# Last layers of a graph network: whole float32 features against a count matrix that GpSimd's queue widens while it loads

## The chip, the cores and the metric

The program runs on one core of a Trainium2 chip. The metric is the device time of one execution in microseconds; lower is better. The kernel before was run three times.

## The reference

A graph of 6250 nodes with 128 features and 106,250 edges (self loops among them) passes through four blocks, each followed by a residual add and a layer norm: an attention layer, a dense block with edge sums, three attention layers, and at the end five layers (GIN) that this case is about:

```python
for l in range(5):
    agg = jax.ops.segment_sum(h[src], dst, num_segments=N)
    rst = h + agg
    x = rst @ W1[l] + b1[l]
    x = jax.nn.relu(_bn(x, bn1_g[l], bn1_b[l]))
    x = x @ W2[l] + b2[l]
    x = jax.nn.relu(_bn(x, bn2_g[l], bn2_b[l]))
    h = jax.nn.relu(_bn(x, bn3_g[l], bn3_b[l]))
```

`_bn` normalises each feature over all nodes. The edges are the same in all five layers.

## The kernel before

The nodes are 49 blocks of 128 (`NB`), padded to 50 (`NBP`). Features live either with nodes on the partitions (`X`, `S`) or with features on the partitions (`XTa`, `XTb`).

**The count matrix.** The segment sum of the last five layers is done as a dense product. `adjacency()` (lines 1493 to 1562) builds, once, how often each source node feeds each destination node. The destinations are cut into 13 windows (`NWIN`) of 504 columns (`WD`; the last has 224), the sources into the 49 blocks, which gives 637 (`NKEY`) panels of 128 x 504. TensorE adds up one-hot products in PSUM (line 1516). DVE makes the one-hots (1523, 1526). ScalarE copies two panels at a time to float16 (1549), zeroes the banks (1551) and stores the pair (1539), in a hardware loop over the pairs. In HBM each panel is 128 rows of 504 float16 values. In the first half of this stage GpSimd gathers rows for another layer on its queue (lines 1196 to 1213).

**One layer** is `neighbours(l)` (from 1564), then `linear`, `relu_norm`, and `split_features(False)` (1783), which turns the result back to nodes on partitions for the next layer. Between phases stands a barrier of all engines (`end_phase`).

- The features are held as three bf16 parts whose sum is the float32 value (`H3`): ScalarE rounds to the first part (1807), DVE subtracts and rounds to the second (1812, 1814), GpSimd subtracts for the third (1817).
- Lines 1586 to 1590 compute 52 sums of features for edges that the matrix leaves out (`extra`, the extra counts), and lines 1591 to 1603 split those into three parts too (`V3`).
- The main loop (1605 to 1630) goes over the windows in two parts: windows 0 to 6 (3528 columns), then 7 to 12 (2744 columns), one PSUM bank for each window. For each of the 49 source blocks it takes one tile of counts (line 1622, the three bf16 parts one after the other) and adds the block's own features by an identity (1625).
- A tile is loaded by SyncE's queue (`load_tile`, 1777), in 7 or 6 panels of 1008 bytes a partition. There are five tile buffers (`NT`), three of them in `XTb`, and the first two tiles of a layer (`KEPT`) are loaded during the phase before. A load waits for the product of the tile five before it.
- Line 1636 adds the extra sums. DVE and ScalarE then evict the windows (1645, 1648). The first dense weights (1583, float32) are multiplied window by window within the second part's matmuls, one window every five blocks, and at the end for the second part; ScalarE adds the bias (1651) and DVE takes statistics.

Before the first layer, `run_hit` is built by an iota and a comparison (1770, 1772) and `split_features(True)` splits `X`. After the fifth layer `feature_to_node` (894) turns the features back with transposes (873), an activation (901) and a copy (907), and a layer norm and the store of the output follow.

Of the kernel before, what the change touches and what calls it, by code (L numbers as in the profile page):

```python
# [19 lines left out]
F32 = mybir.dt.float32  # L20
BF16 = mybir.dt.bfloat16
F16 = mybir.dt.float16
# [59 lines left out]
NT = 5  # L82
# [21 lines left out]
def build(nc, a, out):  # L104
    ctx = ExitStack()
    with ctx:
# [19 lines left out]
        adj = dram("adjacency", (2 * PAIRS, P, WD), F16)  # L126
# [4 lines left out]
        S = sb("state", NBP * C)  # L131
        XTa = sb("xT_a", NP)
        XTb = sb("xT_b", NP)
        steptab = sb("step_table", 3 * KS, I32, 1)
        act_tab = sb("act_table", 2 * KT, I32, 1)
        freetab = sb("free_table", T // TG, I32, 1)
        fresh = sb("new_block", KP)
        src_cols = sb("src_cols", ET)
        dst_cols = sb("dst_cols", ET)
# [6 lines left out]
        Wext = sb("w_ext", 4 * (D + 2))  # L146
# [10 lines left out]
        src_idx = sb("src_idx", ET, I32)  # L157
        step_col = sb("step_col", KJ)
        run_dst = sb("run_dst", 1)
        extra = sb("extra_counts", NV * NBP, F16)  # L160
# [5 lines left out]
        def gsb(name, cols, dt=F32):  # L166
            return gat_only.enter_context(nc.sbuf_tensor(name, [P, cols], dt))
# [31 lines left out]
        for name in ("chain", "load", "load2", "store", "stage", "mm", "evac", "out",  # L199
# [4 lines left out]
                     *[f"ld{h}" for h in range(NT)], *[f"st{h}" for h in range(RG)],  # L204
# [689 lines left out]
        def feature_to_node(src, t, c, func, scale, shift):  # L894
# [15 lines left out]
            end_phase()  # L910
# [582 lines left out]
        def adjacency():  # L1493
# [42 lines left out]

            def store(j, u):
# [4 lines left out]
            def evict(it, us, first=False):  # L1542
                regs = step_regs[act.engine][0:len(us)]
                act.load(regs, pair_last[0:1, bass.ds(it * 4, len(us))])
                for u in us:
                    act.wait_ge(q["product"], act.snap(regs[u], min_val=1, max_val=AK))
                    if not first:
                        act.wait_ge(q[f"st{u}"], it * 16)
# [3 lines left out]
                    if u or not first:  # L1552
                        store(it * 4 + u - 1, (u - 1) % 4)

            evict(0, range(4), True)
            with act.Fori(1, PAIRS // 4) as it:
                evict(it, range(4))
            evict(PAIRS // 4, range(PAIRS % 4))
            store(PAIRS - 1, (PAIRS - 1) % 4)
            for u in range(4):  # L1560
                act.wait_ge(q[f"st{u}"], 16 * (PAIRS // 4 + (u < PAIRS % 4)))
            end_phase(gather_first_layer(TABLES, T))

        def neighbours(l):
# [6 lines left out]
            parts = [range(0, DW), range(DW, NWIN)]  # L1571
            width_of = lambda w: min(WD, NB * P - w * WD)
# [13 lines left out]
            by_block = extra[:, :].rearrange("p (c b) -> p b c", b=NBP)  # L1586
# [4 lines left out]
            dve.wait_ge(q["bcast"], 1)  # L1591
            s = Serial()
            part = lambda t, i: t[0:NV, i * D:(i + 1) * D]
            of_bank = PS[:, 7 * 512:7 * 512 + 3 * D]
            rest, high = rows5[0][0:NV, 0:D], rows5[0][0:NV, D:2 * D]
            s(dve, lambda: dve.tensor_copy(rest, part(of_bank, 0)))
            for i in (1, 2):
                s(dve, lambda: dve.tensor_tensor(rest, rest, part(of_bank, i), ALU.add))
            for i in range(3):
                s(dve, lambda: dve.tensor_copy(part(V3, i), rest))  # L1600
                if i < 2:
                    s(dve, lambda: dve.tensor_copy(high, part(V3, i)))
                    s(dve, lambda: dve.tensor_tensor(rest, rest, high, ALU.subtract))
            n = 0
            for k, ws in enumerate(parts):
                if k:
                    s.wait(pe)
# [256 lines left out]
```

## Time and profile before

| | |
|---|---|
| median of 3 runs | 11149.94 us (11141.5 to 11180.91) |
| the profiled execution's span | 11182.9 us |
| TensorE matmul busy | 6422.3 us (57%) |
| DVE, ScalarE, GpSimd busy | 36%, 36%, 40% |
| DMA, mean | 106 GB/s |

The page's 40 slices show stages. Each digit is a tenth of a slice of 280 us; PEclk is the clock granted to TensorE in tenths of full speed:

```profile
PE   1611112642367787355554555545554989898997
PEclk8555555765578898677776777777777999999998
DMA  4332223534433442133332333233332546464554
```

The last nine slices are the five layers of this case, from about 8690 us on: TensorE is nearly always busy there and at nearly its full clock. The count matrix is built between 2462 and 3674 us. Busy time is a union of overlapping records; mean durations of matmuls are latencies and overlap. A record of a matmul with float32 operands stands twice for each matmul in the program.

### The profile page before, as it was taken

How to read it: one execution, taken by the hardware profiler on the slowest of the kernel's cores; microseconds unless marked ns; L12 is line 12 of the kernel's file. 1: busy time of each engine (PE TensorE's matmuls, PEld its weight loads, DVE VectorE, ACT ScalarE, POOL GpSimd, SP SyncE). 2: the span in 40 equal slices, each digit the busy share in tenths (PEclk: the TensorE clock that was granted, in tenths of full speed). 3: DMA queues.
4: the chain of work that ended last, by engine and by line, in shares of the span. 5: the costliest groups of instructions: out<-in, count | busy, mean ns of one | idle time of the engine just before them, and what ended most of it. 6: DMA issues, size and time to landing. Idle time of an engine off the chain costs nothing. (4 is left out here: it accounts for less than half of the span.)

```text
span 11182.9 us, 142834 instructions
## 1 busy us (share of the span) xinstructions
PE 6422.3 (57%) x34150; PEld 4429.5 (40%) x34151; DVE 4061.9 (36%) x11422; ACT 3980.1 (36%) x8307; POOL 4429.3 (40%) x4465
## 2 busy tenths in 40 slices
PE   1611112642367787355554555545554989898997
PEld 1600001630012575255553555535554444444443
DVE  3800001442278787444444444534445020201112
ACT  2046662002278775344443444434444010101001
POOL 3866667247710000366664666466664000000000
PEclk8555555765578898677776777777777999999998
DMA  4332223534433442133332333233332546464554
GB/s 122 95 88 86 87 85 111 144 104 121 123 120 117 142 133 88 45 72 72 72 71 64 71 72 72 58 76 71 71 72 49 181 146 200 141 202 140 167 173 134
DMA packets 1106637, 1190.87 MB, mean 106 GB/s; under 512 B 118423, under 2 KB 991526, under 8 KB 1105944
## 3 DMA queue, kind: packets, MB, share of 16 engines
q1 hardware_dynamic: 710164, 628.94, 19.0%
q0 software_dynamic: 150784, 336.22, 12.6%
q10 hardware_dynamic: 245444, 222.71, 7.1%
q8 instruction: 122, 2.00, 0.1%
q14 instruction: 123, 1.01, 0.0%
HBM read 973.07 MB, written 216.86 MB: 106 GB/s over the span
## 5 line engine op out<-in xcount | busy, mean ns | idle before, releaser
L1196 POOL DMA_INDIRECT ring<-gat_rows,src_idx x2496 | 2426.2, 972 | 1550.8 <-issue 946.1
L1316 PE MATMUL ps<-ring,xT_b 128*128 x8192 | 1494.4, 339 | 1697.0 <-ACT xT_b L1402 1091.5
L1316 PEld LDWEIGHTS ps<-ring,xT_b 128*128 128x128 f32 x8192 | 1312.4, 243 | 1884.8 <-issue 1883.4
L1394 ACT ACTIVATE xT_a<-xT_a,state 128x514 f32<-128x514 f32 x1024 | 742.6, 725 | 2370.7 <-DVE xT_a L1364 1751.7
L1364 DVE CUSTOM_DVE_ANT_0 xT_a<-ps,mask,xT_a 128x512 f32<-128x512 f32 x1024 | 768.9, 751 | 2241.7 <-remote 1361.7
L1622 PE MATMUL ps<-xT_b,features 128*128 128x504 f16 (+1 forms) x5655 | 1198.3, 367 | 0.0
L690 POOL DMA_INDIRECT by_src<-ring,state x832 | 806.7, 970 | 462.1 <-issue 462.1
L1307 PE MATMUL ps<-ident,s_col 128*128 128x128 f32 x4096 | 750.3, 316 | 214.0 <-issue 129.9
L1622 PE MATMUL ps<-adj_tile,features 128*128 128x504 f16 (+1 forms) x3900 | 827.4, 367 | 0.0
L1046 POOL TENSOR_TENSOR x_nodes<-x_nodes,state 128x1280 f32<-128x1280 f32 x12 | 39.4, 3311 | 1971.2 <-DMA ring<-gathered 1254.2
L1817 POOL TENSOR_TENSOR features<-xT_a,features 128x640 bf16<-128x640 f32 x40 | 56.1, 1402 | 1919.7 <-DVE features L1814 1919.7
L657 PE MATMUL ps<-xT_a 128*128 128x50 bf16 x832 | 184.2, 221 | 1052.2 <-ACT xT_a L646 778.9
L1323 PE MATMUL ps<-ident,xT_b 128*128 128x128 f32 x4096 | 762.1, 319 | 3.9 <-issue 3.6
L1622 PEld LDWEIGHTS ps<-xT_b,features 128*128 128x128 bf16 x5655 | 531.3, 98 | 570.6 <-issue 20.0
L1411 ACT ACTIVATE xT_b<-xT_a,neg 128x514 f32<-128x514 f32 x1024 | 741.3, 724 | 33.1
L1516 PE MATMUL ps<-ring,xT_a 128*128 128x504 bf16 x1104 | 450.1, 499 | 515.5 <-issue 293.9
L1379 DVE SCALAR_TENSOR_TENSOR xT_a<-xT_a 128x514 f32<-128x514 f32 x1024 | 704.4, 688 | 0.0
L1307 PEld LDWEIGHTS ps<-ident,s_col 128*128 128x128 f32 x4096 | 593.5, 165 | 238.4 <-issue 159.0
L1323 PEld LDWEIGHTS ps<-ident,xT_b 128*128 128x128 f32 x4096 | 611.9, 170 | 6.6 <-issue 5.4
L1213 POOL DMA_INDIRECT dl_all<-gat_rows,src_idx x484 | 545.5, 1127 | 147.8 <-issue 147.1
L1402 ACT ACTIVATE xT_b<-ps 128x512 f32<-128x512 f32 x1024 | 597.1, 583 | 16.0 <-PE ps L1323 9.0
L1549 ACT ACTIVATE xT_b<-ps 128x1008 f16<-128x1008 f32 x319 | 319.1, 1000 | 700.4 <-PE ps L1516 398.0
(379 smaller groups left out, 8639.2 us busy)
## 6 DMA issues: line engine op xcount, KB each, us to landing
dl_all<-dloc_rows ACTq DMA_DIRECT2D x1052, 128.0 KB
xT_b<-adjacency SPq DMA_DIRECT2D x145, 882.0 KB, 4.8
xT_b<-adjacency SPq DMA_DIRECT2D x145, 756.0 KB, 4.6
adj_tile<-adjacency SPq DMA_DIRECT2D x100, 882.0 KB
adjacency<-xT_b ACTq DMA_DIRECT2D x319, 252.0 KB
adj_tile<-adjacency SPq DMA_DIRECT2D x100, 756.0 KB
ring<-by_src SPq DMA_DIRECT2D x52, 1040.0 KB
ring<-gathered SPq DMA_DIRECT2D x208, 260.0 KB
```

The costliest lines, as they stand in the source:

```text
L690: pool.indirect_dma_start(by_src[:, :], bass.IndirectOffsetOnAxis(pos[:, g * L1U + u:g * L1U + u + 1], 0), ring[:, b * group + u * RC:b * ...
L1196: pool.indirect_dma_start(ring[:, o:o + RC], None, table[:, :], bass.IndirectOffsetOnAxis(src_idx[:, t * W + u:t * W + u + 1], 0)).then_in ...
L1213: pool.indirect_dma_start(held[h][:, u * RC:(u + 1) * RC], None, gat_rows[:, :], bass.IndirectOffsetOnAxis(src_idx[:, i:i + 1], 0)).then_i ...
L1307: m = pe.transpose(bank(BS + u % 4)[:, w * P:(w + 1) * P], s_col[u % 4][:, w:w + 1].to_broadcast([P, P]), ident[:, :])
L1316: m = pe.matmul(bank(BO + v % 2, R), pw[v % 4][:, w * P:(w + 1) * P], ring[:, w * RC:][:, bass.ds(look(SLOT, u - 7), R)], start=w == 0, st ...
L1323: m = pe.transpose(bank(BP + v % 2)[:, w * P:(w + 1) * P], pt[v % 8][:, w * P:(w + 1) * P], ident[:, :])
L1364: dve.tensor_tensor_reduce(out=m[:, 0:TE], in0=bank(BS + u % 4, TE), in1=mask[u % 4][:, :], scale=1.0, scalar=m[:, TE + 1:TE + 2], op0=ALU ...
L1379: dve.scalar_tensor_tensor(w, w, 0.2, w, ALU.mult, ALU.max).then_inc(q["leaky"], 1)
L1394: act.activation(um[u % 4], sm[u % 8], ACT.Identity, bias=S[:, ER:][:, bass.ds(look(BC, u), 1)]).then_inc(q["act_a"], 1)
L1402: act.activation(pw[v % 4], bank(BP + v % 2, TE), ACT.Copy).then_inc(q["pw_ready"], 1)
L1411: act.activation(pt[v % 8], um[v % 4], ACT.Exp, bias=neg[v % 4][:, :]).then_inc(q["weights"], 1)
L1622: m = pe.matmul(bank(w % 8, width), h, tiles[b][:, j * WD:j * WD + width], start=i == 0 and x == 0, stop=False)
```

## The change

- The features are kept as one float32 array `H` instead of three bf16 parts, and the tiles are float32 too. Line 1622's three matmuls with bf16 features become one with float32 operands; the same for the identity, the extra sums (`V`, `extra_of`, `run_hit`). `split_features` is gone: `feature_to_node` writes `H`, and before the first layer `X` is copied to `H` by three engines.
- The matrix stays float16 in HBM. The tiles are loaded by GpSimd's queue (`pool.dma_start`), which converts float16 to float32 on the way. There are three tile buffers (`NT = 3`), none in `XTb`. Phases that end with such loads wait for them on GpSimd and reset its DMA state (`end_phase(pool_dmas)`).
- The matrix in HBM has one row of 13 x 504 = 6552 values for each source node, so a partition's share of a tile is one run of 7056 or 5488 bytes. A pair of panels that lies in one row is stored by one DMA, in one run of 2016 bytes a partition; a pair that straddles two blocks takes two. ScalarE's loop over the pairs is written out.
- Some arrays (`S`, index tables) move to a region that is freed before the last layers, and `S` is made anew at the end. `extra` is copied to float32 for that.
- Bias and statistics of the first part's windows are issued from within the loop; the order on each engine is as before.

```diff
-NT = 5
+NT = 3
-        adj = dram("adjacency", (2 * PAIRS, P, WD), F16)
+        adj = dram("adjacency", (NB, P, NWIN * WD), F16)
...
             def store(j, u):
                 act.wait_ge(q["evac"], j + 5)
-                act.dma_start(adj[bass.ds(j * 2, 2), :, :].rearrange("k p c -> p k c"), out4[u]
-                              ).then_inc(q[f"st{u}"], 16)
+                keys = [k for k in (2 * j, 2 * j + 1) if k < NKEY]
+                at = [divmod(k, NWIN) for k in keys]
+                if len(at) == 2 and at[0][0] == at[1][0]:
+                    runs = [(at[0], 0, 2)]
+                else:
+                    runs = [(x, c, 1) for c, x in enumerate(at)]
+                for (i, w), c, n in runs:
+                    act.dma_start(adj[i, :, w * WD:(w + n) * WD].rearrange("p (k c) -> p k c", c=WD),
+                                  out4[u][:, c:c + n, :]).then_inc(q[f"st{u}"], 16)
+                    stored[u] += 16
...
-            evict(0, range(4), True)
-            with act.Fori(1, PAIRS // 4) as it:
-                evict(it, range(4))
-            evict(PAIRS // 4, range(PAIRS % 4))
+            for it in range(-(-PAIRS // 4)):
+                us = range(min(4, PAIRS - it * 4))
...
+            of_runs = PS[0:NV, 7 * 512:7 * 512 + D]
             for i in range(NB):
-                m = pe.matmul(PS[0:NV, 7 * 512:7 * 512 + 3 * D], by_block[:, i, :], H3[:, i * 3 * D:(i + 1) * 3 * D],
+                m = pe.matmul(of_runs, extra_of[:, i * NV:(i + 1) * NV], H[:, i * D:(i + 1) * D],
                               start=i == 0, stop=i == NB - 1)
...
                     if n >= NT:
-                        sp.wait_ge(q["product"], n - NT + 1)
+                        pool.wait_ge(q["product"], n - NT + 1)
                     if n >= KEPT:
                         load_tile(i, ws, b)
...
+                    if n == 1:
+                        dve.wait_ge(q["bcast"], 1)
+                        s(dve, lambda: dve.tensor_copy(V[0:NV, :], of_runs))
...
-                    for x in range(3):
-                        h = H3[:, (i * 3 + x) * D:(i * 3 + x + 1) * D]
-                        for j, w in enumerate(ws):
...
+                    h = H[:, i * D:(i + 1) * D]
+                    for j, w in enumerate(ws):
...
+                        v = tiles[b][:, j * WD:j * WD + width]
+                        m = pe.matmul(bank(w % 8, width), h, v, start=i == 0, stop=False)
+                        if lo < hi:
+                            pe.matmul(bank(w % 8)[:, lo - w * WD:hi - w * WD], h, ident[:, lo - i * P:hi - i * P],
+                                      start=False, stop=False)
...
-                    for x in range(3):
-                        m = pe.matmul(bank(w % 8, width), part(V3, x), run_hit[0:NV, w * WD:w * WD + width],
-                                      start=False, stop=x == 2)
-                    m.then_inc(q["summed"], 1)
+                    pe.matmul(bank(w % 8, width), V[0:NV, :], run_hit[0:NV, w * WD:w * WD + width],
+                              start=False, stop=True).then_inc(q["summed"], 1)
...
-            end_phase()
+            end_phase([(f"ld{b}", 16 * len([n for n in range(KEPT, 2 * NB) if n % NT == b])) for b in range(NT)])
...
+        tiles = [nsb(f"adj_tile{i}", DW * WD) for i in range(NT)]
...
-            sp.dma_start(tiles[b][:, 0:len(ws) * WD].rearrange("p (w c) -> p w c", c=WD),
-                         adj[i * NWIN + ws[0]:i * NWIN + ws[-1] + 1, :, :].rearrange("w p c -> p w c")
-                         ).then_inc(q[f"ld{b}"], 16)
+            n = cuts[ws[0] // DW][1]
+            pool.dma_start(tiles[b][:, 0:n], adj[i, :, ws[0] * WD:ws[0] * WD + n]).then_inc(q[f"ld{b}"], 16)
...
+        loading = preload()
+        thirds = [slice(i * NBP * D // 5, j * NBP * D // 5) for i, j in ((0, 2), (2, 4), (4, 5))]
+        act.activation(H[:, thirds[0]], X[:, thirds[0]], ACT.Copy)
+        dve.tensor_copy(H[:, thirds[1]], X[:, thirds[1]])
+        pool.tensor_copy(H[:, thirds[2]], X[:, thirds[2]])
+        end_phase(loading)
...
             layer(l)
-            split_features(False)
+            loading = preload()
+            feature_to_node(XTb, H, D, ACT.Relu, aff[:, 0:1], aff[:, 1:2], loading)
```

## Rows read from the trace of the kernel before

**Rows 1.** The page, busy time: us, share of the span, instructions.

```profile
PE 6422.3 (57%) x34150; PEld 4429.5 (40%) x34151; DVE 4061.9 (36%) x11422; ACT 3980.1 (36%) x8307; POOL 4429.3 (40%) x4465
```

**Rows 2.** Windows of one layer: stretch, length, busy (x), PEclk, DMA share, GB/s.

```profile
8684.40:8695.40 11.00, 10.94 (x50) 8.52 (x51) 0.17 (x1) 0.00 (x0) 0.00 (x0) 0.73 0.84 260
8695.40:8919.00 223.60, 223.60 (x1132) 105.40 (x1131) 2.50 (x10) 0.00 (x0) 0.00 (x0) 1.00 0.63 192
8919.00:8923.60 4.60, 4.60 (x23) 1.92 (x23) 2.05 (x3) 1.73 (x3) 0.00 (x0) 1.00 0.61 174
8923.60:9103.70 180.10, 180.10 (x979) 91.77 (x979) 5.48 (x8) 4.81 (x8) 0.00 (x0) 1.00 0.63 190
9103.70:9107.30 3.60, 3.60 (x20) 1.64 (x19) 1.36 (x2) 1.41 (x3) 0.00 (x0) 1.00 0.00 0
9107.30:9175.90 68.60, 34.95 (x95) 17.18 (x94) 49.62 (x93) 41.15 (x62) 14.02 (x10) 0.67 0.08 27
```

**Rows 3.** Waits of TensorE's side in 8695 to 9104: total, times, longest.

```profile
PEld ps L1622 <- issue: 4.2, 15, 0.4
```

**Rows 4.** DMA in 8710 to 8900: packets, MB, share; one issue group.

```profile
q1 hardware_dynamic: 37940, 37.58, 65.1%
...
xT_b<-adjacency SPq DMA_DIRECT2D x25, 882.0 KB, 4.8
```

**Rows 5.** By line and form, 8695 to 9104: busy us, mean ns, idle before.

```profile
L1622 PE MATMUL ps<-xT_b,features 128*128 128x504 f16 x1044 | 237.8, 376 | 0.0
L1622 PE MATMUL ps<-adj_tile,features 128*128 128x504 f16 x720 | 164.5, 376 | 0.0
```

**Rows 6.** Line 1583's instructions: min/median/max ns, first and last start.

```profile
L1583 PE MATMUL ps<-xT_a,w_static x130: 352/586/690, 8975.7 to 11086.7; 128*128 128x504 f32 x120, 128*128 128x224 f32 x10
```

**Rows 7.** Timeline around line 1583 in the second half: start, length.

```profile
8975.41 0.47 PE L1622 MATMUL ps<-xT_b,features 128*128 128x504 f16 x2
...
8975.72 1.02 PE L1583 MATMUL ps<-xT_a,w_static 128*128 128x504 f32 x2
...
8976.58 0.38 PE L1622 MATMUL ps<-xT_b,features 128*128 128x504 f16 x1
```

**Rows 8.** Timeline, short float32 matmuls in a row.

```profile
8571.35 2.09 PE L1316 MATMUL ps<-ring,xT_b 128*128 x16
```

**Rows 9.** Timeline, the split of the features, first and next phase's record.

```profile
9153.79 1.73 ACT L1802 ACTIVATE rows<-xT_b,affine 128x640 f32<-128x640 f32 x2 [1.71 <-PEq L1796]
...
9175.92 0.86 ACTq L1567 DMA_DIRECT2D w_static<-in_L_gnn_W  x2
```

**Rows 10.** Timeline, the last turn back to nodes.

```profile
11127.76 1.73 ACT L901 ACTIVATE rows<-xT_b,affine 128x640 f32 x2 [1.77 <-PEq L896]
...
11138.56 1.64 DVE L907 COPY state<-ps 128x640 f32 x2 [0.24 <-PE ps L873]
11140.95 9.86 POOL L1046 TENSOR_TENSOR x_nodes<-x_nodes,state 128x1280 f32<-128x1280 f32 x3 [481.67 <-SPq L220]
```

**Rows 11.** Timeline, the first split.

```profile
8658.25 6.37 ACT L1807 ACTIVATE features<-x_nodes 128x640 bf16<-128x640 f32 x10 [11.96 <-PEq L220]
...
8684.46 10.99 PE L1588 MATMUL ps<-features,extra_counts 128*52 128x384 bf16 x49 [66.41 <-PEq L220]
```

**Rows 12.** GpSimd's lines: its direct DMA issues, busy us, mean ns.

```profile
L1205 POOL DMA_DIRECT2D gathered<-dl_all x121 | 71.0, 588 | 1.8 <-DMA dl_all<-gat_rows,src_idx 1.6
```

**Rows 13.** DMA in 2600 to 2900: packets, MB, share of 16 engines.

```profile
q0 software_dynamic: 10991, 28.17, 34.6%
```

**Rows 14.** Line 1539's instructions: min/median/max ns, first and last start.

```profile
L1539 ACTq DMA_DIRECT2D adjacency<-xT_b x319: 378/378/401, 2467.9 to 3675.3; - x160
```

**Rows 15.** Waits in 2480 to 3050: total, times, longest.

```profile
ACT xT_b L1549 <- issue: 265.8, 38, 11.9
```

**Rows 16.** The stage of the count matrix as one window, columns as rows 2.

```profile
2462.00:3674.00 1212.00, 582.00 (x1472) 156.43 (x1472) 629.09 (x1836) 629.62 (x637) 526.56 (x589) 0.66 0.39 119
```

More of the change, by code:

```diff
@@ L145, in build @@
         Wst = sb("w_static", 8 * D)
-        Wext = sb("w_ext", 4 * (D + 2))
         vec = sb("vectors", 128)
@@ L1584, in first_weights, with evict, bias_and_stats @@
                           ).then_inc(q["mm"], 1)
[L1586 removed]
+            def evict(ws):
+                for w in ws:
+                    if w % 2 == 0:
+                        dve.wait_ge(q["summed"], w + 1)
+                        dve.tensor_copy(window(w), bank(w % 8, width_of(w))).then_inc(q["evac"], 1)
+                    else:
+                        act.wait_ge(q["summed"], w + 1)
+                        act.activation(window(w), bank(w % 8, width_of(w)), ACT.Copy).then_inc(q["out"], 1)
+            def bias_and_stats(w):
+                act.wait_ge(q["mm"], w + 1)
+                act.activation(window(w), bank(5 + w % 2, width_of(w)), ACT.Identity, bias=gv["b1"]
+                               ).then_inc(q["stage"], 1)
+                stats_of(XTa, w, WD, min(WD, N - w * WD), "stage", w + 1)
+            of_runs = PS[0:NV, 7 * 512:7 * 512 + D]
+            s = Serial()
             for i in range(NB):
[L1588 removed]
+                m = pe.matmul(of_runs, extra_of[:, i * NV:(i + 1) * NV], H[:, i * D:(i + 1) * D],
                               start=i == 0, stop=i == NB - 1)
             m.then_inc(q["bcast"], 1)
[L1591 to L1603, printed above, removed]
             n = 0
             for k, ws in enumerate(parts):
[L1606 to L1607 removed]
                 for i in range(NB):
@@ L1790, in split_features, with preload @@
+            pool.dma_start(tiles[b][:, 0:n], adj[i, :, ws[0] * WD:ws[0] * WD + n]).then_inc(q[f"ld{b}"], 16)
+        def preload():
             for b in range(KEPT):
                 load_tile(b, range(0, DW), b)
-            for b in range(KEPT):
-                sp.wait_ge(q[f"ld{b}"], 16)
-            whole = (lambda g: of(X, D, g)) if first else bank_of
-            if not first:
-                pe.sem_inc(q["mm"], 2 * GB)
-                dve.sem_inc(q["evac"], 2)
-                turn()
@@ L1799, in split_features @@
-            for g in range(groups + 1):
-                if g < groups and not first:
-                    act.wait_ge(q["mm"], (g + 1) * GB)
-                    act.activation(rows5[g % 2][:, :], XTb[:, g * GB * P:(g + 1) * GB * P], ACT.Relu, bias=aff[:, 1:2],
-                                   scale=aff[:, 0:1]).then_inc(q["stage"], 1)
-                if g:
-                    if not first:
-                        act.wait_ge(q["mm"], (g + 2) * GB)
-                    act.activation(of(H3, 3 * D, g - 1), whole(g - 1), ACT.Copy).then_inc(q["act_a"], 1)
```

123 lines of the change are left out of this document (54 added, 69 removed).

## The prediction

> **What bounds the kernel now.** I read the page's busy shares first. TensorE is the busiest engine, but only 57% of the span [rows 1], so an average says little and the stage that changes has to be read alone. The last five layers are that stage. The windows cut at the boundaries of one of them [rows 2] show what a layer is made of: 11.0 us for the sums of the extra edges, 223.6 us for the first half of the nodes (seven windows of 504 columns), 4.6 us for the extra edges of that half, 180.1 us for the second half (five windows of 504 and one of 224), 3.6 us, and 68.6 us of dense layers, norms and the splitting of the features. In both halves TensorE is busy for the whole window at a granted clock of 1.00 (its 2.4 GHz level), while DVE, ScalarE and GpSimd are nearly idle and the DMA engines are busy for 0.63 of the time. The waits of that stretch confirm it: nothing makes a matmul wait for a tile; the largest wait of TensorE's side is 4.2 us of weight loads [rows 3]. So 404 us of each layer are a pure stream of columns through TensorE, and the tiles (882 KB, 4.8 us to land [rows 4]) are hidden behind it.
>
> How fast is that stream? In the first half each of 49 blocks sends 3528 columns, and the self loops send another 3528 in all, three times over because the features are three bf16 parts: 3 x (49 x 3528 + 3528) = 529,200 columns in 223.6 us, 0.4225 ns each. The second half is 3 x (49 x 2744 + 2744) = 411,600 columns, and seven weight matmuls of line 1583 stand in it. 180.1 - 7 x 0.86 (below) = 174.1 us, 0.423 ns each. The by-line rows [rows 5] show the same matmuls; their mean of 376 ns is a latency, with neighbours overlapping, and is no price.
>
> **The change, part by part.**
>
> *Three bf16 passes become one float32 pass.* What does a float32 window cost in such a stream? Line 1583 multiplies float32 windows of 504 columns in the midst of the bf16 ones. Two records stand for each window: 130 records [rows 6] for 5 layers x 13 windows. From the first of them to the next bf16 matmul is 8976.58 - 8975.72 = 0.86 us [rows 7], 4 x 504 columns at 0.427 ns. So a float32 column costs four bf16 columns, and four replace three. At 0.423 ns the first half is 4 x 176,400 columns = 298.4 us (+74.8), the second 4 x 137,200 = 232.1 us (+58.0), and the matmuls of line 1636 go from 8.2 to 10.9 us (+2.7). That is +135.5 us a layer, +678 us in five. With 0.427 ns it is +701; I take 678, since a long stream amortises the change of type. All of it lies on the path, for TensorE has no idle time to absorb it.
>
> *Sums of the extra edges (line 1588).* 49 matmuls of 384 bf16 columns in 10.9 us [rows 2] become 98 float32 records of 128 columns. By columns that is 98 x 107 = 10.5 us; by the nearest short float32 matmuls, 16 in 2.09 us [rows 8], 12.8 us; at the lower clock (0.73 in this window) up to 21 us. I take +1 us a layer, +5; the ends are -2 and +50.
>
> *Splitting the features goes.* From ScalarE's first activation of the split (9153.79) to the next layer's first record (9175.92) is 22.1 us [rows 9]. The function that takes its place runs once already, at the end: 11127.76 to 11140.95, 13.2 us [rows 10]. -8.9 us, four times: -36 us. Cover is needed for the two preloaded tiles, which the end of that phase now waits for; their price is below (about 12 to 14 us for two, so just hidden). The first split took 26.2 us [rows 11]. In its place stand copies (10 x 640 columns took 6.4 us on ScalarE, so a share of two fifths is under 3 us) and, ending last, the preload at 14 us: -12. Two more DVE copies of 2600 columns, near 3 us each by the same row, and a barrier of 2 us: +8. Together -4 us.
>
> *The DVE chain that split the extra sums* ran beside the first half, as the 2.5 us of DVE in that window: hidden before, hidden after, 0. The order of the evictions on DVE and ScalarE does not change either, since each engine's own order is the same: 0.
>
> *Who loads the tiles, and with what.* SyncE's queue carried nothing else; now GpSimd's queue does, and GpSimd has no work in the halves (0.00 us [rows 2]). One issue on it cost 588 ns [rows 12], once per 5 to 6 us, with nothing queued behind it but the next load. Waiting for the landed tiles and the reset at two phase ends a layer: no row shows it alone; a plain phase end took 0.75 us from the end of DVE's last copy to the next phase's first add [rows 10], so I bound it at 0 to 3 us each and take 0.5 x 10 = +5. With three buffers instead of five a tile's load is issued when the tile three before it is done, so it has the time of two tiles, 12.2 us in the first half and 9.7 us in the second.
>
> *Do the loads still hide?* This is the open term. A tile is now written as 128 x 3528 x 4 = 1.806 MB, and TensorE eats it in 298.4 / 49 = 6.09 us; in the second half 1.405 MB in (232.1 + 6.0) / 49 = 4.86 us. That asks for 297 and 289 GB/s on the written side. No transfer of the trace changes type, so I bound it. Lower end of the cost: the engines pay for the bytes read, 149 GB/s, less than now: 0. Next: they pay for bytes written at the pace of the present tiles, 192 GB/s for 0.63 busy [rows 2], 37.58 MB for 65.1% of 190 us [rows 4], both 304 GB/s: 5.9 and 4.6 us a tile, just hidden: 0. The software queue's own row, 28.17 MB for 34.6% of 300 us [rows 13], gives 271 GB/s: 6.66 and 5.18 us, 49 x 11.84 = 580 us against 536: +44 a layer, +220. Upper end: widening halves the pace to 152 GB/s: 49 x (11.9 + 9.2) = 1034 us, +498 a layer, +2490. I take 0, because the nearest row is that of the same tiles, and rows of 7056 bytes in one piece should not be slower than seven of 1008.
>
> The Trainium skill (DMA: Bandwidth & Descriptors, "Anatomy of one DMA") fits a GpSimd-issued transfer as 2.0 us plus bytes / 436 GB/s; by it, counted on written bytes, a tile takes 4.1 us beyond the fixed part and the sum would be the same. The trace has 4.8 us for 882 KB, where that fit gives 4.1.
>
> *The count matrix (stage at 2462 to 3674).* The 319 pair stores of 378 ns [rows 14] become 343: 24 pairs straddle a row of 6552 and need two. If ScalarE were the bound all through, +9 us. Against that, each store has one run per partition instead of two and the loop over pairs is written out. ScalarE idled 265.8 us on "issue" there [rows 15], yet TensorE and DVE idle in the same stretch too, and ScalarE is busy for only 630 of 1212 us [rows 16]. Ends -266 and +30; I take 0.
>
> **Sum.** 678 + 5 - 36 - 4 + 5 + 0 + 0 = +648 us. The profiled execution spans 11182.9 us and would become 11831; it stands 0.3% above the median of the runs, 11149.9, to which the sum gives 11798. Forecast 11800 us. A measurement here can tell about 0.5% from no change.
>
> **The rivals.**
>
> A. *The loads become the bound, mildly* (the software queue's 271 GB/s): +220, 12,020 us. For it: the margin at 304 GB/s is only 3% and 5%, and two tiles ahead leave little slack. Against it: one run per partition.
>
> B. *Widening is slow in the DMA engines*: at half pace, 14,290 us; at 230 GB/s, 7.85 and 6.11 us a tile, 684 us, +738, 12,540. For it: nothing in the trace bounds a transfer that changes type. TensorE would then idle between tiles, and its clock with it: the window with TensorE busy for 35 of 68.6 us shows 0.67.
>
> C. *Not slower: a float32 window in a stream costs two passes*, the two records taking 0.21 us each as bf16 ones do. Then the halves shrink to 149 and 116 us, -135 a layer, 10,450 us. The change turns at 0.64 us a window (three bf16 passes); the row says 0.86 [rows 7].
>
> D. *The count matrix gains its stalls back*: if the stores and ScalarE's loop were what held the stage, up to -266: 11,530 us. It would need -648 to reach no change, more than half of that stage's 1212 us.
>
> E. *DVE locks GpSimd's descriptor writing while tiles are preloaded.* DVE copies stand in the phase of 13.2 us; were both loads held until it ended, the -36 us would go: 11,835 us. The Trainium skill (SBUF — State Buffer, section "SBUF: two separate sides") states this rule for DVE's two-port operations; no row here shows it, and it is within the range.
>
> **How the numbers follow.** The forecast with its own small terms (and E) 0.56; A 0.18; B 0.18; C 0.03; D 0.05. The range must drop no more than 2 in 10. Downwards I take 11,700 (part of D); upwards it takes in A and the light edge of B: 12,350. Left out: most of B, C, and the far end of D, about 0.2. Slower by over 0.5%: 0.96; within 0.5%: 0.01; faster: 0.03.
>
> **What would show it.** The two halves should read near 298 and 238 us a layer with TensorE busy throughout and a clock of 1.00, and no wait of a matmul on a tile. Waits for a load there mean A or B, and landing times over 12 us; halves near 150 us mean C. The phase after the norms should last 13 us, and the count-matrix stage 1212 us. I am wrong if the DMA engines cannot write 297 GB/s while they widen.

## The result, and the profile after

The kernel before takes 11162.35 us (median of 4 runs, 11141.5 to 11180.91) beside 11779.01 us after the change (4 runs, 11740.01 to 11784.36). The ratio is 1.0551 with an interval of 1.0513 to 1.0589: slower by 617 us. The forecast was 11800 us.

The page of the changed kernel, whose profiled execution spans 11774.2 us. The rows are each engine's busy time, and of the forty slices TensorE, its granted clock and the DMA engines:

```profile
PE 7044.2 (60%) x30840; PEld 4726.6 (40%) x30841; DVE 4002.5 (34%) x11320; ACT 3948.3 (34%) x8258; POOL 4609.1 (39%) x4906
...
PE   1611113622477874555545554555579898989997
...
PEclk7555555855698996777767776777889999999998
DMA  4332234533334431322223332332257575757575
...
L1636 PE MATMUL ps<-adj_tile,features 128*128 128x504 f32 (+1 forms) x6370 | 2640.5, 569 | 0.0
...
L1794 POOL DMA_DIRECT2D adj_tile<-adjacency x490 | 259.3, 529 | 2785.9 <-PE ps L1636 2459.3
```

The last eleven slices are the last layers: TensorE is at seven to nine tenths of each, with a dip at the end of a layer, and line 1636, the product with the count matrix, has no idle time before it. Before, the same product had 9555 matmuls of 16-bit operands in five layers; now there are 6370 records of float32, two for each window.

The same layer as in [rows 2], cut at the same boundaries (columns as there; the last is GB/s of the DMA engines, the one before it their busy share):

```profile
8637.50:8935.20 297.70, 297.70 (x757) 137.88 (x755) 0.28 (x1) 0.00 (x0) 25.33 (x48) 1.00 0.77 289
8935.20:8941.30 6.10, 6.10 (x16) 2.53 (x15) 2.05 (x3) 1.77 (x3) 0.53 (x1) 1.00 0.63 230
8941.30:9179.00 237.70, 237.70 (x657) 120.41 (x657) 5.48 (x8) 4.76 (x7) 24.28 (x46) 1.00 0.75 272
9179.00:9183.80 4.80, 4.80 (x14) 2.17 (x13) 1.37 (x2) 1.45 (x3) 0.00 (x0) 1.00 0.00 0
```

The first half went from 223.6 to 297.7 us and the second from 180.1 to 237.7 us. TensorE is busy for the whole of both, at a granted clock of 1.00, its 2.4 GHz level. The only new work is GpSimd's: 48 and 46 loads, 25 us of issuing in each half, beside TensorE.

The waits of that stretch (engine, line, what it waited for: total us, times, longest):

```profile
POOL adj_tile L1794 <- PE ps L1636: 489.3, 95, 18.5
...
PEld ps L1636 <- issue: 249.0, 1069, 0.7
```

GpSimd waits for TensorE, 95 times: the loader is the one with time to spare. TensorE's side has no wait on a load. Its 249 us are idle time between weight loads, for which the profile names no releaser; TensorE never stopped beside them, so they cost nothing ([rows 3] had 4.2 us of them).

The edges of a layer in the timeline (start, length, engine, what; idle time in brackets), from the end of one layer to the next:

```profile
8624.90 12.74 PE L1609 MATMUL ps<-features,extra_wide 128*52 128x128 f32 x98 [58.55 <-PEq L221]
...
8637.56 1.11 PE L1636 MATMUL ps<-adj_tile,features 128*128 128x504 f32 x2
...
9230.06 1.73 ACT L902 ACTIVATE rows<-xT_b,affine 128x640 f32 x2 [1.75 <-PEq L897]
...
9243.61 0.82 ACTq L1574 DMA_DIRECT2D w_static<-in_L_gnn_W  x2
...
9243.97 0.53 POOL L1794 DMA_DIRECT2D adj_tile<-adjacency  x1 [12.71 <-SPq L221]
...
9247.29 13.85 PE L1609 MATMUL ps<-features,extra_wide 128*52 128x128 f32 x98 [5.78 <-issue]
...
9261.07 1.11 PE L1636 MATMUL ps<-adj_tile,features 128*128 128x504 f32 x2
```

The same edges in the kernel before:

```profile
8695.38 0.39 PE L1622 MATMUL ps<-adj_tile,features 128*128 128x504 f16 x1
...
9179.40 11.00 PE L1588 MATMUL ps<-features,extra_counts 128*52 128x384 bf16 x49 [8.87 <-issue]
9190.33 0.39 PE L1622 MATMUL ps<-adj_tile,features 128*128 128x504 f16 x1
```

From one layer's first product at 8637.56 to the next one's at 9261.07 is 623.5 us. Before it was 494.95 us, from 8695.38 to 9190.33. The difference, +128.6 us a layer, is to the tenth the forecast of 135.5 + 1 - 8.9 + 1. That it meets so exactly is partly luck: the terms behind it were off by up to 2 us and cancel (below). Over the whole part, from the first sums of extra edges to the end, before took 11182.9 - 8684.4 = 2498.5 us and after 11774.2 - 8624.9 = 3149.3 us: +650.8.

The profiled span grew by 591 us only, because the layers begin 59.5 us earlier (8624.9 against 8684.4). Of that, 7.8 us are the shorter preparation. The other 52 us lie ahead of it, and the changed kernel's run on another chip, the eighth experiment, tells whether they belong to the change.

### The profile page after: what moved, and what is told of

It is laid out like the page before. It is cut to its first block and busy times, and to the rows that moved or that the text cites. A ratio compares the mean times of both kernels' runs of the same rounds, so it can differ in the third digit from the quotient of the medians.

```text
span 11774.2 us, 134861 instructions
## 1 busy us (share of the span) xinstructions
PE 7044.2 (60%) x30840; PEld 4726.6 (40%) x30841; DVE 4002.5 (34%) x11320; ACT 3948.3 (34%) x8258; POOL 4609.1 (39%) x4906
## 5 line engine op out<-in xcount | busy, mean ns | idle before, releaser
L1636 PE MATMUL ps<-adj_tile,features 128*128 128x504 f32 (+1 forms) x6370 | 2640.5, 569 | 0.0
L1636 PEld LDWEIGHTS ps<-adj_tile,features 128*128 128x128 f32 x6370 | 1186.2, 190 | 1248.4 <-issue 1248.4
L1794 POOL DMA_DIRECT2D adj_tile<-adjacency x490 | 259.3, 529 | 2785.9 <-PE ps L1636 2459.3
```

Source lines behind the costliest of these rows:

```text
L1636: m = pe.matmul(bank(w % 8, width), h, v, start=i == 0, stop=False)
```

## The experiments

The first four ran together on one chip, where the kernel before takes 11156.65 us (11056.53 to 11197.7, 7 runs). The other five ran on two further chips, where it takes 9675 and 9676 us. The last layers are as long there as here; what differs is told with the eighth.

Where two theories spoke of the same 648 us, I called them "passes" (a float32 column costs four bf16 columns on TensorE) and "loads" (the widening transfers, or GpSimd's issuing of them, take part of it).

### A fourth bf16 pass in the kernel before

```diff
-                    for x in range(3):
+                    for x in (0, 1, 2, 2):
```

The same edit stands in the loop over the extra sums. Everything else is the kernel before, its plain loads by SyncE included.

> The kernel before, with the third bf16 part of the features multiplied twice, so four passes instead of three in line 1622, in the identity matmuls and in the extra sums (the third part is counted twice in the output). Loads stay on SyncE's queue, nothing is widened, the split stays. Theory (the float32 product costs what four bf16 passes cost, and nothing else of the change matters much): each pass is 176,400 + 137,200 columns at 0.423 ns plus 2.7 us, 135 us a layer, +677 us, 11,840 us, and the two halves read near 298 and 238 us as after the change. Rival (float32 operands cost less than four passes and the loads from GpSimd's queue make up the rest): this kernel is slower than the changed one by clearly more than the 60 us that the changed one saves elsewhere.

11756.95 us (11684.11 to 11813.46, 4 runs), a ratio of 1.0556 (1.0468 to 1.0643), the same as that of the change. The two halves of its first layer:

```profile
8605.90:8904.00 298.10, 298.10 (x1509) 140.56 (x1508) 2.50 (x10) 0.00 (x0) 0.00 (x0) 1.00 0.47 144
...
8910.10:9148.20 238.10, 238.10 (x1300) 121.66 (x1299) 5.48 (x8) 4.77 (x7) 0.00 (x0) 1.00 0.48 144
```

1509 bf16 matmuls fill 298.1 us where the change has 757 float32 records in 297.7. A float32 pass is four bf16 passes within 0.2%, and that alone gives the size of the halves.

### No loads in the layers

```diff
-                    if n >= NT:
-                        pool.wait_ge(q["product"], n - NT + 1)
-                    if n >= KEPT:
+                    if KEPT <= n < NT:
                         load_tile(i, ws, b)
```

> The changed kernel without the tile loads of the main loop: the three tiles of blocks 0 to 2 are loaded and used again for all 49 blocks and both parts (so the counts are wrong). TensorE's work is the same. Theory (the widening loads are hidden): the halves stay at 297.7 and 237.7 us, the time is 11,780 within 0.5%. Rival (the loads hold TensorE back a little everywhere, by waits that a union of records doesn't show, or by SBUF traffic): it gets faster by more than 0.5%, 11,720 or less.

11675.89 us (11634.96 to 11704.32, 4 runs), a ratio of 1.0484 (1.0409 to 1.0559). The halves:

```profile
8546.00:8843.60 297.60, 297.60 (x755) 137.86 (x754) 0.28 (x1) 0.00 (x0) 0.00 (x0) 1.00 0.00 0
...
8849.80:9087.40 237.60, 237.60 (x657) 120.36 (x656) 5.48 (x8) 4.76 (x7) 0.00 (x0) 1.00 0.00 0
```

With the DMA engines at 0.00 of their time, a half is 0.1 us shorter than with 1.8 MB arriving every 6 us. From the first product to the last it takes 11572.9 - 8546.0 = 3026.9 us, the changed kernel 11666.9 - 8637.6 = 3029.3. The loads cost 2.4 us in five layers, 0.1%. The median is 103 us below that of the change all the same, which is more than the 0.5% that the rival asked for. But nearly all of it lies before the layers, which begin at 8546.0 and not at 8637.5, where the two programs do the same. The halves decide for the theory.

### More bytes to widen, until it shows

```diff
                         load_tile(i, ws, b)
+                        pool.dma_start(XTb[:, b * MORE:(b + 1) * MORE], adj[i, :, 0:MORE]).then_inc(q[f"ld{b}"], 16)
```

MORE is 2132 columns. The bytes go to a place that nothing reads.

> The changed kernel with a second widening load of 2132 columns beside each tile load, into a region that nothing reads; each tile waits for both. A first-half tile writes 5660 columns of float32, 2.898 MB, in the 6.09 us that TensorE needs, a second-half tile 2.497 MB in 4.86 us. Theory (the DMA engines pay for written bytes, at the 378 GB/s that the changed kernel's row gives, 71.41 MB for 78.7% of 240 us): 7.67 and 6.61 us a tile, 49 x 14.27 = 699 us a layer against 536, +163 a layer, +815, 12,590 us. Rival 1 (the share of busy time overstates the load, and the engines have more room): clearly less, down to no change. Rival 2 (widening has an own limit just above the present 298 GB/s): 9.6 and 8.3 us a tile at 303 GB/s, +340 a layer, +1700, 13,480 us.

12035.14 us (12010.38 to 12078.71, 4 runs), a ratio of 1.0814 (1.0736 to 1.0892). First the windows of both halves, then the largest wait on a load on TensorE's side there, then the queue in 8550 to 8830 (packets, MB, share of 16 engines):

```profile
8511.90:8842.20 330.30, 309.00 (x755) 135.00 (x754) 0.28 (x1) 0.00 (x0) 50.79 (x96) 1.00 1.06 414
...
8848.40:9132.90 284.50, 250.81 (x657) 117.47 (x656) 5.48 (x8) 4.77 (x7) 48.68 (x92) 0.99 1.06 409
```

```profile
PEld ps L1638 <- DMA xT_b<-adjacency: 105.6, 89, 2.9
```

```profile
q0 software_dynamic: 11810, 118.85, 109.0%
```

This is what rivals A and B would have looked like: a wait on a load before nearly every block (89 waits for 98 blocks), TensorE's busy time falling behind the window, GpSimd issuing twice as much. The loads are the bound here, and 118.85 MB in 280 us are 424 GB/s. My expectation was 815 us and the main loop grew by 3429.4 - 3029.3 = 400. I had worked out 378 GB/s from the changed kernel's own queue (71.41 MB in 240 us at a share of 0.787), and the chip writes 424: rival 1 of the expectation is right. The share is at fault: it reads 1.06 and 1.09 here, so it is no fraction of a capacity. TensorE's clock stayed at 1.00 and 0.99 with these gaps, so they cost their own length and no more.

### The old panels under GpSimd's queue

```diff
-        adj = dram("adjacency", (NB, P, NWIN * WD), F16)
+        adj = dram("adjacency", (2 * PAIRS, P, WD), F16)
...
-            pool.dma_start(tiles[b][:, 0:n], adj[i, :, ws[0] * WD:ws[0] * WD + n]).then_inc(q[f"ld{b}"], 16)
+            pool.dma_start(tiles[b][:, 0:len(ws) * WD].rearrange("p (w c) -> p w c", c=WD),
+                         adj[i * NWIN + ws[0]:i * NWIN + ws[-1] + 1, :, :].rearrange("w p c -> p w c")
+                         ).then_inc(q[f"ld{b}"], 16)
```

The stores and ScalarE's loop go back to those of before.

> The changed kernel with the count matrix in panels of 504 columns again, as before the change (ScalarE's stores and its loop over the pairs too); GpSimd's queue loads and widens 7 or 6 panels a partition. Theory (the loads have room): a partition's share becomes 7 runs; at the 304 GB/s of the kernel before a first-half tile takes 5.9 us of 6.09, a second-half tile (3024 columns here, the pad is loaded too) 5.1 us of 4.86, so the first half stays at 298 us and the second is at most 250: between 11,780 and 11,850. Rival (GpSimd writes the list of runs itself, and seven times as many take longer: one issue of 527 ns becomes 3 us or more, and short runs are slower): the loads come late in both halves, 12,000 us or more, and the rows of 6552 are what makes the widening load affordable.

11729.55 us (11678.93 to 11780.25, 4 runs), a ratio of 1.0532 (1.0451 to 1.0614). The halves, and then the issue of one load here and in the changed kernel (min/median/max ns, first and last start):

```profile
8607.10:8904.70 297.60, 297.60 (x755) 137.85 (x754) 0.28 (x1) 0.00 (x0) 44.04 (x48) 1.00 1.09 289
...
8910.90:9148.50 237.60, 237.60 (x656) 120.33 (x656) 5.48 (x8) 4.77 (x7) 37.78 (x46) 1.00 1.13 300
```

```profile
L1787 POOL DMA_DIRECT2D adj_tile<-adjacency x490: 821/878/1532, 8580.9 to 11624.7; - x164
```

```profile
L1794 POOL DMA_DIRECT2D adj_tile<-adjacency x490: 527/527/1201, 8612.1 to 11653.1; - x164
```

The 878 ns are the middle between two kinds: the 48 issues of the first half take 44.04 us, 0.92 us each with seven pieces, and the 46 of the second 37.78 us, 0.82 each with six. So seven pieces of 1008 bytes for each partition instead of one of 7056 make the issue 0.92 us instead of 0.53 and lift the busy share from 0.77 to 1.09 at the same 289 GB/s. The time of the halves does not move, and the main loop takes 11638.5 - 8607.1 = 3031.4 us. So the rows of 6552 are not what hides the loads. And a share above 1 stands here with no wait at all. It is made up of the time that each packet took, and nothing keeps that sum below the span.

### The rows alone, in the kernel before

```diff
-            sp.dma_start(tiles[b][:, 0:len(ws) * WD].rearrange("p (w c) -> p w c", c=WD),
-                         adj[i * NWIN + ws[0]:i * NWIN + ws[-1] + 1, :, :].rearrange("w p c -> p w c")
-                         ).then_inc(q[f"ld{b}"], 16)
+            n = sum(min(WD, NB * P - w * WD) for w in ws)
+            sp.dma_start(tiles[b][:, 0:n], adj[i, :, ws[0] * WD:ws[0] * WD + n]).then_inc(q[f"ld{b}"], 16)
```

With it come the 343 stores and ScalarE's written-out loop of the change.

> The kernel before with one part of the change: the count matrix in rows of 6552 (stores of a pair in one run, ScalarE's loop over the pairs written out) and tiles loaded by SyncE's queue in one run of 7056 or 5488 bytes a partition, still float16. Three bf16 passes and the split stay. Theory (the layout helps the DMA engines and nobody waits for them): the main loop does not move, the DMA share in it falls from 0.63 to about 0.5 at the same or fewer bytes; the count-matrix stage stays within 20 us of 1212; the time is 11,160 within 0.3%. If the DMA engines pay for written bytes, plain rows show the pace of the widening ones, about 378 GB/s at full share; if widening costs its own, plain rows are clearly faster than that. Rival (the 60 us by which the changed kernel is ahead when the last layers start come from this part): 11,100 to 11,130 us.

On this chip before takes 9674.73 us (9667.77 to 9681.75, 15 runs) and this kernel 9664.03 (9657.26 to 9675.57, 11 runs): a ratio of 0.9989 (0.998 to 0.9998), 11 us quicker and just outside its own noise. The halves:

```profile
7181.10:7404.70 223.60, 223.60 (x1132) 105.40 (x1131) 2.50 (x10) 0.00 (x0) 0.00 (x0) 1.00 0.58 191
...
7409.40:7589.40 180.00, 180.00 (x977) 91.69 (x977) 5.48 (x8) 4.77 (x7) 0.00 (x0) 1.00 0.55 172
```

They are those of before to 0.1 us. The queue in 7200 to 7390 (packets, MB, share of 16 engines):

```profile
q1 hardware_dynamic: 5997, 37.54, 60.3%
```

By bytes over share that would be a pace of 328 GB/s, neither the 304 of the panels nor the 378 of the widening loads. The expectation meant to read from it what the engines pay for, and it cannot be read so: the last experiment moves such rows at 418. The count-matrix stage, from its first product to its last, takes 2732.0 - 2050.4 = 681.6 us, where the next experiment, with the old loop on the same chip, takes 2750.2 - 2048.8 = 701.4. So the loop and the stores give 20 us there, not the 266 of rival D. On the chip of the result they give none that shows: 1205 us after, 1206.5 before. There the same stage takes 500 us more, and what holds it there was not found; the rows do not touch it.

### Two float16 parts instead of three bf16 parts

The experiments say that the passes are all that the stage costs. If so, the way to use them is fewer 16-bit ones.

```diff
-        H3 = sb("features_3", NBP * 3 * D, BF16)
-        V3 = sb("extra_3", 3 * D, BF16)
+        H3 = sb("features_2", NBP * 2 * D, F16)
+        V3 = sb("extra_2", 2 * D, F16)
...
-                    for x in range(3):
+                    for x in range(2):
...
-                dve.tensor_tensor(rest[g % 2], whole(g), of(H3, 3 * D, g), ALU.subtract).then_inc(q["evac"], 1)
-                dve.wait_ge(q["evac"], g + (1 if first else 3))
-                dve.tensor_copy(of(H3, 3 * D, g, D), rest[g % 2]).then_inc(q["act_b"], 1)
+                dve.tensor_tensor(of(H3, 2 * D, g, D), whole(g), of(H3, 2 * D, g), ALU.subtract).then_inc(q["evac"], 1)
```

GpSimd's third part goes.

> The kernel before with the features in two float16 parts (11 bits of mantissa each) instead of three bf16 parts: two passes in line 1622, in the identity matmuls and in the extra sums; the split's third step on GpSimd goes, and DVE writes the second part in one operation. Theory (time follows the passes): -135 us a layer for the pass and a few us a layer for the shorter split (22 us to about 17), -677 - 25, 10,460 us; the tiles must then be loaded in 2/3 of the time: 882 KB in 3.04 us and 756 KB in 2.4 us, 297 and 323 GB/s, against a pace of 304 at full share, so the loads may become the bound. Rival (they do): halves of 149 and 116 us grow to 150 to 155 and 125 to 130, 10,510 to 10,560 us. If a float16 pass costs more than a bf16 one, the halves are longer with no wait on a load.

8955.73 us (8947.51 to 8960.81, 4 runs), a ratio of 0.9255 (0.9241 to 0.9269) to before: 719 us quicker. The halves:

```profile
7169.50:7318.60 149.10, 149.10 (x756) 70.26 (x754) 1.50 (x6) 0.00 (x0) 0.00 (x0) 1.00 0.94 289
...
7321.80:7443.80 122.00, 122.00 (x657) 61.83 (x656) 5.48 (x8) 4.98 (x8) 0.00 (x0) 1.00 0.88 282
```

149.1 us is two thirds of 223.6 to 0.1 us. The second half is 122.0 and not the 116 of the expectation, which forgot the seven float32 windows of line 1583: 7 x 0.86 = 6.0 us, and they do not shrink. TensorE now eats the plain tiles at 289 and 282 GB/s and still never waits.

### Two parts and rows together

The two edits above in one kernel.

> The kernel before with two float16 parts of the features and with the count matrix in rows of 6552 (ScalarE's loop written out, SyncE's queue loads one run a partition, still float16). Theory: with two parts TensorE never waited for a load, so the rows can only bring what they brought with three parts, 0.1%: the two halves stay at 149 and 122 us, and the time is that of two parts alone, 0.925 of before, within 0.3%. Rival (with the tiles asked for in 2/3 of the time, shorter runs did cost something, or the count-matrix stage gains): 0.915 or less.

8950.93 us (8945.25 to 8953.82, 4 runs) where before takes 9676.41 (9667.71 to 9682.75, 7 runs): 0.9249 (0.9234 to 0.9265). It beats both kernels, by 7.5% and, by the next run, by 1371 us. The rows add 5 us at most to the two parts.

### The changed kernel again, on the quick chip

> The changed kernel once more, beside these. Stages that GpSimd's gathers set took 1500 us less on the chip of the last two runs, the last layers the same. Theory (the change costs 128.6 us a layer and nothing before the layers): +640 to +650 us in absolute terms on either kind of chip, less what varies in the stages before; the ratio is about 1.067 where before takes 9675 us, 1.057 where it takes 11160. Rival (the stages before the layers really gain 50 to 60 us by the change): +590 us on the quick chip too, where those stages vary by a few us only.

10322.0 us (10317.83 to 10324.82, 4 runs), a ratio of 1.0667 (1.065 to 1.0685): +645.6 us. The sum of the prediction was +648. Here is where the two chips differ; the first row of each pair is of this run, the second of the changed kernel in the result (min/median/max ns, first and last start):

```profile
L1317 PE MATMUL ps<-ring,xT_b x8192: 272/275/578, 2799.7 to 7071.3; 128*128 x200
...
L1636 PE MATMUL ps<-adj_tile,features x6370: 352/586/690, 7187.5 to 10212.6; 128*128 128x504 f32 x181, 128*128 128x224 f32 x19
```

```profile
L1317 PE MATMUL ps<-ring,xT_b x8192: 272/275/579, 3691.8 to 8520.8; 128*128 x200
...
L1636 PE MATMUL ps<-adj_tile,features x6370: 352/586/690, 8637.6 to 11666.9; 128*128 128x504 f32 x181, 128*128 128x224 f32 x19
```

The products with the count matrix take 3025.1 us here and 3029.3 there. The attention layers, whose rows GpSimd gathers, end 1449.5 us earlier, and the gathers themselves are no quicker (by line: busy us, mean ns of one, then idle before them and what ended it; this run, and the changed kernel in the result):

```profile
L1197 POOL DMA_INDIRECT ring<-gat_rows,src_idx x2496 | 2410.0, 966 | 1002.9 <-issue 998.9 <-SPq L1173 3.3 <-DMA ring<-gat_rows,src_idx 0.6
```

```profile
L1197 POOL DMA_INDIRECT ring<-gat_rows,src_idx x2496 | 2418.2, 969 | 1538.7 <-issue 942.8 <-SPq L1173 595.9
```

Not all of the 1449.5 us fall into these layers: their first product starts 892.1 us earlier (2799.7 against 3691.8), and from there to the last they are 557.4 us shorter. In that stretch GpSimd waits 596 us for SyncE's queue there and 3 us here, at the same price of a gather. A larger wait differs too, that of DVE (this run, and the changed kernel in the result):

```profile
L1365 DVE CUSTOM_DVE_ANT_0 xT_a<-ps,mask,xT_a 128x512 f32<-128x512 f32 x1024 | 765.5, 748 | 582.3 <-PE ps L1308 460.2 <-issue 94.7 <-DVE mask L1347 17.2
```

```profile
L1365 DVE CUSTOM_DVE_ANT_0 xT_a<-ps,mask,xT_a 128x512 f32<-128x512 f32 x1024 | 769.1, 751 | 2227.8 <-remote 1303.4 <-PE ps L1308 766.7 <-issue 130.3
```

There it waits 1303 us for something that the profile calls remote and does not name, and here not at all. That gathers set the time of these layers on the slow chips is therefore not shown. The four executions on the first chips that share the changed kernel's program up to the last layers (the change, no loads, more loads, old panels but for its stores) have their last product of attention at 8520.8, 8428.6, 8394.8 and 8489.4 us; the two that share that of before (before, the fourth pass) at 8573.2 and 8483.9. So those stages vary by 90 to 126 us from one execution to another, and the 52 us by which the changed kernel came early lie within that. On the quick chips they vary less, and there the change gains nothing ahead of the layers: the last product of attention starts at 7071.3 us here and at 7067.0 in the kernel with two float16 parts, whose program is that of before up to the last layers.

### Plain loads until they show

```diff
                         load_tile(i, ws, b)
+                        sp.dma_start(S[:, b * MORE // 2:(b + 1) * MORE // 2].bitcast(F16), adj[i, :, 0:MORE]
+                                     ).then_inc(q[f"ld{b}"], 16)
```

This is the kernel of two parts and rows, with MORE at 2640 columns.

> The kernel with two float16 parts and rows of 6552, with a second plain load of 2640 float16 columns beside each tile load, into a region that nothing reads; each tile waits for both. A first-half tile moves 0.903 + 0.676 = 1.579 MB in the 3.04 us that TensorE needs (519 GB/s), a second-half tile 1.378 MB in 2.49 us. The widening loads saturated at 430 GB/s of written bytes, 215 GB/s of read bytes. Theory (the engines pay for written bytes, and widening costs nothing beside them): plain loads saturate near the same 430 GB/s: 3.67 and 3.20 us a tile, halves of 180 and 157 us against 149 and 122. Rival (widening has a price of its own, plain loads are quicker than 430 written): halves near 150 and 125 us. Other rival (reads from HBM limit plain loads, which read twice as much for the same written bytes): halves above 190 and 165 us.

9268.4 us (9263.33 and 9273.48, 2 runs), a ratio of 0.9579 (0.956 to 0.9598). The queue in 7200 to 7330, and a wait in the first half:

```profile
q1 hardware_dynamic: 9958, 54.32, 101.4%
```

```profile
PE ps L1631 <- DMA state<-adjacency: 21.8, 38, 0.7
```

And the two halves:

```profile
7153.30:7331.00 177.70, 155.85 (x756) 67.48 (x756) 1.50 (x6) 0.00 (x0) 0.00 (x0) 1.00 1.02 419
7334.06:7493.74 159.68, 129.24 (x657) 58.37 (x657) 5.48 (x8) 5.04 (x8) 0.00 (x0) 1.00 0.98 403
```

TensorE waits for loads again, and 54.32 MB in 130 us are 418 GB/s. The halves of 177.7 and 159.7 us are those of the theory (180 and 157) and of neither rival. By the same view the widening loads ran at 424 GB/s of bytes written (212 of bytes read). Once the loads are the bound, widening in the DMA engines costs what its written bytes cost and nothing beyond that these two runs show.

## Why the prediction came out right

*The passes.* Forecast: +74.8, +58.0 and +2.7 us a layer from 0.86 us for one float32 window of line 1583 [rows 7]. Measured: +74.1 (297.7 - 223.6), +57.6 (237.7 - 180.1) and +2.7 (6.1 + 4.8 - 4.6 - 3.6). That is 134.4 against 135.5. The row held because it stood in the same kind of stream, with bf16 windows before and after it, and because I took it from start to start and not as a duration: the median record of the new stream says 586 ns, yet a window is not two of them, 1172 ns, for 350 windows in 297.7 us are 0.85 us each. The Trainium skill (FP8 and Floating Point Precision, "TensorE Precision Notes") states four passes of the array for true float32; the trace agrees in the price, with 757 records in 297.7 us beside 1509 bf16 ones in 298.1. Rival C (two passes) asked for a first half of 149 us and is ruled out; its 116 us for the second half also left out line 1583's windows.

*The loads.* Forecast: 0. Measured: 0.5 us a layer. The 0 was right and its working was not. I took 304 GB/s as the capacity, from bytes over busy share [rows 2, 4], found a margin of 3 to 5%, and gave rivals A and B 0.36 between them. The step that failed is the division. Under pressure the queues move 418 and 424 GB/s and their share reads 1.01 to 1.09; the old panels under GpSimd's queue move 300 GB/s at a share of 1.13 with no wait, where the division would allow 265; and in [rows 13] 94 GB/s already read 0.35. The margin is 424 against 297 GB/s, 30%. The share gives no bound of that kind, and the range reached up to 12350 for nothing. That the sum had 0 for this term all the same owes something to luck: by the pace of [rows 13] it would have been +220. The Trainium skill (DMA: Bandwidth & Descriptors, "Specifications") gives 435 GB/s as the ceiling of the fabric through which the 16 engines reach SBUF. Both saturated queues are within 4% of it, so the sentence of the prediction that rested on the neighbouring fit of that page, and which the sum did without, was nearer to the chip than the sum's own bound.

*The extra sums (L1609).* Forecast +1 us, measured 12.7 us in the first layer and 13.8 in the second (9247.29 to 9261.07) beside 10.9 (9179.40 to 9190.33): +2.9. The estimate lay between 10.5 and 12.8, and the upper one, from short float32 matmuls [rows 8], was the better row. I shaded it down without a reason. On the other side of the sum, from the first activation of the turn back to the next extra sums 9247.29 - 9230.06 = 17.2 us passed, and before 9179.40 - 9153.79 = 25.6: 8.4 us gained, where the forecast had 8.9 for the phase itself.

*Barriers.* Forecast +1 us a layer for the waits on landed tiles and the resets. From the last extra sums to the turn back, 46.3 us passed after and 46.5 before, with one of the two phase ends in it; the other is within the 8.4 us above. Together: 134.4 + 2.9 - 8.4 - 0.2 = 128.7 a layer, where the periods say 128.6 and the forecast said 128.6.

*The first preparation.* From the first work on the features to the first product, 8637.56 - 8611.64 = 25.9 us, before 8695.38 - 8658.25 = 37.1, with extra sums that are longer now. To the start of the extra sums the preparation gained 7.8 us, where I had 4: counted from the last instructions of the layer norm ahead, 8684.46 - 8644.48 = 40.0 us became 8624.90 - 8592.75 = 32.2. The phase itself was 13.3 us (8624.9 - 8611.64), as the forecast 14 had it; what comes before it grew by 5 us, and I had added 8 for two DVE copies and a barrier.

*The count matrix (D).* Forecast 0, measured 0 on the chip of the result (1205 against 1206.5 us) and -20 us in the stage itself on the quicker one, of which nothing is left where the last layers begin. ScalarE's 265.8 us of "issue" [rows 15] were idle time that the stage had anyway.

*DVE locking GpSimd (E).* In the turn back it had no occasion: GpSimd's two issues, begun at 9230.20, take 1.05 us, and DVE's first copy starts at 9232.52. The gain that E would have taken away came, 8.4 us a layer. But in the first preparation a load was issued beside one of DVE's copies from SBUF to SBUF:

```profile
8611.65 1.49 DVE L1805 COPY features<-x_nodes 128x2560 f32<-128x2560 f32 x1 [0.74 <-PEq L221]
8612.06 1.20 POOL L1794 DMA_DIRECT2D adj_tile<-adjacency  x1 [4.84 <-PEq L221]
```

This issue takes 1.20 us, the longest of all 490, whose median is 0.53, and it ends at 8613.26, 0.12 us after the copy. That is what the rule weighed under E would look like. It happens once in the execution. The phase ends when the preloaded tiles have landed, so it can account for at most 0.7 of its 13.3 us.

*Where the total came from.* The sum said +648; the last layers and their preparation gave +650.8 - 7.8 = +643 in the profile, the quick chip +645.6. The medians of the result say +617, and the difference is within the 90 us by which the stages ahead of them vary there. The forecast of 11800 is 21 us above the median; that it is so near is luck, since those stages alone move it by more.

## What to carry to other kernels

Price a stream of matmuls from start to start of neighbours in a stream like it: the records' durations overlap, and the rate of one float32 window in the midst of 16-bit ones gave five layers to 1%. A DMA busy share is no utilisation; to learn what the engines can still take, add bytes until something waits for them. And when float32 operands are split into 16-bit parts, TensorE's time follows the number of parts: whole float32 counts as four, so it loses to three and loses far more to two. Two float16 parts hold fewer bits than three bf16 parts and have float16's narrow range; whether a kernel may use them depends on its values.

## What the runs showed of the hardware

- Widening 16-bit values to float32 in GpSimd's queue runs at 424 GB/s of written bytes when it is the bound; a plain load by SyncE's queue at 418 GB/s.
- The DMA busy share reads 0.77, 1.09 and 1.13 at 289 to 300 GB/s with TensorE never waiting, and 1.06 at 414 GB/s with TensorE waiting before nearly every block. With whole rows it rises with the load (0.77 at 289, 1.06 at 414 GB/s); with small pieces it stands at 1.09 at 289 already. So it is comparable only between loads of the same shape.
- GpSimd issues a load of 128 rows in 0.53 us, one of 128 x 6 pieces in 0.82 us and one of 128 x 7 in 0.92 us. One issue that met a DVE copy from SBUF to SBUF took 1.20 us.
- The stages ahead of the last layers differ between chips: the kernel before takes 9675 us on two of them and 11157 on another, with the last layers alike to 0.1%. GpSimd's gather instructions take 966 and 969 ns in both; DVE waits 1303 us for a remote releaser on the slow chip of the result and not at all on the quick one. What that is was not settled.
